# Twenty-four slot tiles of a mixture-of-experts layer computed in pairs of one expert, with a transposed first layer

## The reference

```python
# xf: 2048 tokens x 256; E = 8 experts, hidden width H = 512, top 2; S = 2 shared experts
sh = gelu(einsum('nd,sdh->snh', xf, sw1) + sb1)
shared_out = (einsum('snh,shd->nd', sh, sw2) + sb2.sum(0)) / S
gates = xf @ router_w + router_b
topv, topi = top_k(gates, 2)
probs = softmax(topv)
comb = einsum('nke,nk->ne', one_hot(topi, E), probs)
h = gelu(einsum('nd,edh->enh', xf, w1) + b1[:, None, :])
y = einsum('enh,ehd->end', h, w2) + b2[:, None, :]
x = x + tanh(g_ffn) * (shared_out + einsum('ne,end->nd', comb, y))
```

## Time and profile before

| | us |
|---|---|
| median of 3 runs | 387.39 |
| least and most | 387.09, 388.18 |
| profiled execution | 387.97 |
| its span | 386.1 |
| TensorE busy in it | 379.8 |
| VectorE, ScalarE, GpSimd busy | 280.9, 249.4, 221.1 |

### The profile page before, as it was taken

One profiled execution on the slowest core, in us unless ns is written; L12 is line 12 of the kernel. 1 busy time (PEld: TensorE's weight loads), 2 busy tenths in 40 slices (PEclk: granted clock), 3 DMA queues, 4 the chain that ended last, 5 costly groups with the idle time before them and its releaser, 6 DMA issues.

```text
span 386.1 us, 9097 instructions
## 1 busy us (share of the span) xinstructions
PE 379.8 (98%) x2725; PEld 354.3 (92%) x2726; DVE 280.9 (73%) x627; ACT 249.4 (65%) x600; POOL 221.1 (57%) x261
## 2 busy tenths in 40 slices
PE   8999999999999999999999999999999999999996
PEld 7898989999999899999999989999999999999995
DVE  5798799988988998797889885445554455445386
ACT  2766545646755635888869757776667666777850
POOL 8366656788788762577872345555555555552200
PEclk9999999999999999999999999999999999999999
DMA  7990000001000066003930112222222222221397
GB/s 230 306 321 3 2 14 29 16 22 33 14 14 27 17 230 247 14 4 70 274 98 1 36 49 70 83 70 83 69 82 73 78 71 79 75 75 42 87 355 254
DMA packets 32539, 35.89 MB, mean 93 GB/s; under 512 B 9531, under 2 KB 26365, under 8 KB 32509
## 3 DMA queue, kind: packets, MB, share of 16 engines
q1 hardware_dynamic: 27664, 25.21, 21.9%
q0 software_dynamic: 4768, 10.28, 8.7%
q10 hardware_dynamic: 76, 0.02, 0.0%
HBM read 25.79 MB, written 9.59 MB: 92 GB/s over the span
## 4 chain that ended last, share of the span: by engine, by line
PE 92%; DVE 3%; POOL 2%; ACT 1%; issue 1%; DVEq 0%; POOLq 0%
PE psum L1348 14%; PE psum L1395 13%; PE psum L1206 12%; PE psum L1229 11%; PE psum L1166 10%; PE psum L1122 9%; PE psum L1414 4%; PE psum L1089 3%; PE psum L1337 2%; PE psum L1008 2%; PE psum L1046 2%; PE psum L1070 2%; PE psum L1154 1%; PE psum L988 1%; PE psum L1186 1%
## 5 line engine op out<-in xcount | busy, mean ns | idle before, releaser
L1883 DVE COPY hs<-psum 128x512 f32<-128x512 f32 x39 | 27.0, 691 | 56.4 <-PE psum L1395 56.4
L681 POOL DMA_INDIRECT xsl<-y_rows,table x39 | 38.3, 982 | 47.5 <-PE psum L1337 36.2
L688 POOL DMA_INDIRECT y_tok<-ysl,table x39 | 38.6, 990 | 31.8 <-ACT ysl L949 31.5
L966 ACT ACTIVATE hr<-psum,b_cur 128x128 f32<-128x128 f32 x156 | 44.4, 372 | 3.0 <-DVE hr_lo L1873 1.2
L662 POOL DMA_INDIRECT names<-named,pos x32 | 37.8, 1181 | 12.8 <-issue 7.9
L949 ACT ACTIVATE ysl<-psum,table 128x256 f32<-128x256 f32 x39 | 18.5, 475 | 38.7 <-PE psum L1348 38.7
L615 POOL TENSOR_TENSOR Eb<-Eb,rinv 128x512 f32<-128x512 f32 x32 | 33.5, 1065 | 13.1 <-DVE rinv L1604 13.1
L825 ACT ACTIVATE yTb<-psum 128x256 f32<-128x256 f32 x16 | 6.2, 385 | 42.6 <-PE psum L1186 42.6
L1348 PE MATMUL psum<-w_hi,hr_hi 128*128 x156 | 28.0, 301 | 0.0
L1873 DVE TENSOR_TENSOR hr_lo<-hr,hr_hi 128x512 fp32r<-128x512 f32 x39 | 26.6, 682 | 1.8 <-ACT hr_hi L970 1.8
L1395 PE MATMUL psum<-w_hi,xsT_hi 128*128 x78 | 27.6, 436 | 0.0
(11 more groups left out here) (248 smaller groups left out, 1169.7 us busy)
## 6 DMA issues: line engine op xcount, KB each, us to landing
w_raw<-in_L_ffn_w SPq DMA_DIRECT2D x2, 4096.0 KB, 18.1
y_got<-y_tok SPq DMA_DIRECT2D x8, 512.0 KB, 7.6
xs_all<-in_x SPq DMA_DIRECT2D x4, 512.0 KB, 12.3
sw_raw<-in_L_ffn_sw SPq DMA_DIRECT2D x2, 1024.0 KB, 13.9
y_rows<-ybuf SPq DMA_DIRECT2D x16, 128.0 KB, 1.7
out<-xs_all SPq DMA_DIRECT2D x3, 512.0 KB, 3.2
wq_sb<-in_L_xattn_Wq SPq DMA_DIRECT2D x2, 512.0 KB, 6.5
wo_sb<-in_L_xattn_Wo SPq DMA_DIRECT2D x1, 1024.0 KB, 14.2
```

The lines of the kernel that those rows point to most:

```text
L681: nc.gpsimd.indirect_dma_start(xsl[:, s % 2, :], None, y_rows, bass.IndirectOffsetOnAxis(ap=table[:, s, 0:1].bitcast(I32), axis=0)).then_i ...
L688: nc.gpsimd.indirect_dma_start(y_tok, bass.IndirectOffsetOnAxis(ap=table[:, s, 1:2].bitcast(I32), axis=0), ysl[:, s % 2, :], None).then_in ...
L966: last = nc.scalar.activation(hr[:, m, :], bank[4 + par][:, m * P:(m + 1) * P], ACT.Gelu, bias=b1_cur[:, par, m:m + 1])
```

## The change

The slot tiles are sorted otherwise: 15 single tiles and 24 tiles in 12 pairs ("doubles") whose two tiles belong to one expert. Six singles run first, then the 12 doubles, then nine singles. `entry(s)` gives the place in the tables.

In a double:

- TensorE takes w1 as the fixed operand and the turned x of both tiles (256 columns) as the moving one, so that h comes out transposed and needs no turn: 24 matmuls (L1586), no transposes of h, no hs copy. x of both tiles is turned into one bank by 4 transposes (`turn_wide`, L1479). The second layer of the pair before takes 24 matmuls (`give_wide`, L1492), in two halves.
- The weights of the pair's expert are first copied by VectorE into w1_cur (`move_weights`, L2095; 128x1024 for the high and as much for the low part, two buffers), two doubles ahead.
- ScalarE makes four gelus of 128x256 in two halves; hr2 holds one half, so each half's rounded copy (`kept`) and low part (`half_left`) come before the next half's gelus.
- GpSimd's order is written out anew, with gathers up to three doubles ahead.

w1_cur lies where the low part of the shared experts' weights (sw_s[1]) was. SP writes this part to DRAM (2 MB, `sw_lo_kept`) ahead of the doubles and reads it back in four pieces at the end; TensorE waits for it before the late shared experts. The routing tables get the sorting into pairs, and their running sum stands behind `columns_rest(2)` now. A few semaphores are merged, and the counters are six instead of five.

```diff
+DOUBLES = (TOK * TOPK // P - E) // 2
+SINGLES = SLOT_TILES - 2 * DOUBLES
+DOUBLE0 = 6
+SINGLE1 = DOUBLE0 + 2 * DOUBLES
...
+        w1_cur = at_words("w1_cur", [P, 2, 2, KD, HID], AT_SW + 2 * SW_WORDS, F32R)
...
+            sp.wait_ge(sw_ready, SW_PIECES)
+            sp.dma_start(sw_lo_kept[:, :], sw_s[1][:, :].bitcast(F32)).then_inc(sw_moved, 16)
+
             sp.wait_ge(routed_all, 1)
...
+                n = s - (SLOT_TILES - BACK)
+                if n >= 0:
+                    sp.wait_ge(h_psum, SINGLE1 + n)
+                    piece = slice(n * 2 * SW_WORDS // BACK, (n + 1) * 2 * SW_WORDS // BACK)
+                    sp.dma_start(sw_s[1][:, piece].bitcast(F32), sw_lo_kept[:, piece]).then_inc(sw_moved, 16)
...
+            for d in range(1, DOUBLES):
+                for n in range(2):
+                    if d + 3 < DOUBLES:
+                        gather(tile_of(d + 3) + n)
+                    scatter(tile_of(d - 1) + n)
+                if d == DOUBLES - 2:
+                    for n in range(2):
+                        gather(SINGLE1 + n)
+                if d == DOUBLES - 1:
+                    gather(SINGLE1 + 2)
+            for s in range(SINGLE1 + 1, SLOT_TILES):
                 if s + 2 < SLOT_TILES:
                     gather(s + 2)
-                if s >= 3:
-                    scatter(s - 3)
+                scatter(s - 3)
...
+                def gelus(h):
+                    act.wait_ge(h_psum, s + (h + 1))
+                    act.wait_ge(ht_lo, s + h)
+                    for m in range(2):
+                        last = nc.scalar.activation(hr2[:, m, :], bank[2 + 2 * par + h][:, m * 2 * P:(m + 1) * 2 * P], ACT.Gelu,
+                                                    bias=b1_cur[:, par, 2 * h + m:2 * h + m + 1])
+                    last.then_inc(ht_raw, 1)
+
+                def kept(h):
+                    act.wait_ge(ht_raw, s + (h + 1))
+                    if d == 0:
+                        act.wait_ge(ye_psum, DOUBLE0 - 1 + h)
+                    elif h == 0:
+                        act.wait_ge(half_used, s - DOUBLE0)
+                    else:
+                        act.wait_ge(ye_psum, s)
+                    nc.scalar.activation(hr2_hi[:, 2 * h:2 * h + 2, :], hr2[:, :, :], ACT.Copy).then_inc(ht_hi, 1)
+
+                act.wait_ge(b1_ready, s + 2)
+                gelus(0)
+                if d == DOUBLES - 1:
+                    turned(SINGLE1, 0)
+                else:
+                    turned_wide(s + 2, 1 - par)
+                kept(0)
+                gelus(1)
+                kept(1)
+                output(s - 2, 0)
+                output(s - 1, 1)
...
+            def double(d, par, s, j):
+                pe.wait_ge(xt_lo, s + 2)
...
+                pe.wait_ge(w1_moved, s + (2 - DOUBLE0))
+                for m in range(HC):
+                    n, half = 0, m // 2
+                    for x_part, w_part in ((xsT2_hi, 0), (xsT2_hi, 1), (xsT2_lo, 0)):
+                        for k in range(KD):
+                            last = nc.tensor.matmul(bank[2 + 2 * par + half][:, (m % 2) * 2 * P:(m % 2 + 1) * 2 * P],
+                                                    w1_cur[:, par, w_part, k, m * P:(m + 1) * P],
+                                                    x_part[:, k, :], start=(n == 0), stop=(n == 3 * KD - 1))
+                            n += 1
+                    if m % 2 == 1:
+                        last.then_inc(h_psum, 1)
...
+            def move_weights(par, n):
+                nc.vector.tensor_copy(w1_cur[:, par, n, :, :],
+                                      w1_s[n][:, at(expert(2 + par)), :, :].rearrange("p a k n -> p (a k) n").bitcast(F32)
+                                      ).then_inc(w1_moved, 1)
...
+                if d == 0:
+                    move_weights(1, 1)
+                half_left(0)
+                if more:
+                    dve.wait_ge(h_psum, s + 2)
+                    move_weights(par, 0)
+                half_left(1)
+                if more:
+                    move_weights(par, 1)
```

## The result

The changed kernel took 394.46 us (median of 4, 391.98 to 399.48) beside 387.24 (387.02 to 388.18) of the kernel before: a ratio of 1.016, 95% interval 1.0122 to 1.0198. The ratio leaves out the longest execution, which counts as a slow one. The kernel is slower by 1.6%, where 386.0 and a range of 381.5 to 391.0 were forecast. The profiled execution took 391.98, its span is 390.2; against the profiled execution of before that is 4.0 more, where the sum said 1.4 less. The other executions are longer still; how far the traces explain that is told at the end.

The account below looks back on a forecast made before the run. TensorE, busy 98% of the span, was taken as the bound. 387.97 - 9.6 + 1.1 + 4.8 + 0.8 + 1.2 + 0.3 = 386.6, less 0.58 to the median: 386.0 us, range 381.5 to 391.0.

Parts of the forecast that it names:

- hole of 4.8 us: Leaving the doubles: TensorE waits 4.8 us for tile 30's gather, which stands behind two scatters on GpSimd; bounds 4.0 to 5.8.
- the landing of tile 7's gather: Entering the doubles: the gather lands 2.8 us after its start, making TensorE wait +0.3 us.
- the three waits behind the hole: After the doubles: outputs of 26 and 27 +0.8, gather of 32 +0.5, first singles +0.7 us; together 1.0 to 2.8.
- What bounds the kernel: Kernel before: TensorE, busy 98% of the span, 3.48 us per slot tile; an edit pays by shortening its list.
- Part 1: TensorE's list in a double: a pair falls from 6.98 to 6.18 us, gaining 9.6 us over 12 doubles.
- Part 2: Whether another engine sets the doubles' period of 6.18 us: none is full, costed at nothing.
- copy and circle: In doubles: weights' copy 0.69 us, ScalarE-VectorE circle through hr2 5.76 with it, 0.4 to spare; 6.29 with a 1.22 copy.
- The collision: Rival in the doubles: weights' copies and GpSimd's DMAs delay each other, the circle becomes the bound; 391 us, chance 0.23.
- Part 3: Entering the doubles: +0.3 us for tile 7's gather, +0.8 for a late copy of weights; +1.1, bounds 0.6 to 1.5.
- Part 4: Leaving the doubles: GpSimd's order makes a 4.8 us wait for tile 30, then further waits of 0.8, 0.5 and 0.7.
- Part 5: Ahead of routed tiles: longer routing tables delay w2's load by 1.35 us, ScalarE's wait 4.6; +0.3, bounds 0 to 1.5.
- the fall of the clock: Rival behind the hole: TensorE's clock drops to 1.2 GHz after the idle time; 388.4 us, at most 390.7, chance 0.15.

Follow-up runs that it names:

- after_again: The changed kernel, unchanged, run and profiled again: 392.97 us, 1.012 of the kernel before.
- hole_filled_b: Changed kernel plus 52 unread TensorE transposes where it waits for tile 30, gather as late: 390.46 us, 1.007 of the kernel before.
- all_three: gathers_first plus gather of 32 earlier, outputs of 28 and 29 later, two weight copies elsewhere on VectorE: 383.22 us, 0.9876 of kernel before; 401.49 on a slower chip.
- gathers_first: Changed kernel with GpSimd's gathers of tiles 30 and 31 ahead of the scatters of 24 and 25: 402.95 us on a slower chip, 385.89 when rerun elsewhere.

## Why the prediction was wrong, step by step

Three steps of the prediction failed. The largest was left at nothing: the sum has a hole of 4.8 us and takes the clock behind it as 1.00. The other two were sized too small: the landing of tile 7's gather at the entrance, and the three waits behind the hole.

- **What bounds the kernel**: right. TensorE's list was the bound before, and it is in the doubles.
- **Part 1**, the list of a double: right, 6.19 against 6.18 and 0.12 for a matmul, but the last digit is luck. Four transposes of x take 0.35 and not 0.28, as the four transposes of h had shown (272.07 to 272.43, 0.36), and the second layer 2.96 and not 3.02. The gain is 12 x (6.96 - 6.19) = 9.2 instead of 9.6, since a tile had cost 3.48, not 3.49.
- **Part 2**, copy and circle: right. The copies took 0.70 and 0.71, estimated 0.69; the reserve was 0.27, estimated 0.4. The collision, the rival on the slower side, cost TensorE nothing, though it can be seen on GpSimd: four DMAs that began while a copy ran (234.70, 243.54, 259.25, 263.38) took 1.09 to 1.27 in place of 0.96 to 0.98, and ended 0.8 to 0.9 after the copy. The copies never took more than 0.745, also those that began with or just before a scatter. GpSimd gave way and had the slack for it, as the prediction's argument against this rival said. The rule of the Trainium skill in "SBUF — State Buffer", section "SBUF: two separate sides", would have made the two exclude each other for a whole instruction. The trace agrees for a DMA that begins during a copy; it does not for a copy that begins together with a DMA (265.34 for both, copy 0.72, scatter 0.98).
- **Part 3**, the entrance, +1.1: too small. By distances of starts 1.6 for the gather of tile 7 (predicted 0.3), 0.9 for the copy (0.8) and 0.4 at 260.0: 2.9. The 0.7 that TensorE waited there for a copy is the only wait that the profile names inside the twelve doubles, and part 3 had costed it. The term that failed is the landing: I took the median of 2.8 where the row gave 4.2 as the longest, and it was 4.0 at the one gather that had no reserve; with the packet of instructions at another time, in after_again, there was no wait at all.
- **Part 4**, the way out: the hole right in place, cause and size, 4.9 between starts against 4.8, each station of GpSimd as computed (314.95, 316.21, 317.47, where the end of double 10 at 312.53 and the computed 2.33, 3.61, 4.89 make 314.86, 316.14, 317.42). The three waits behind it came to 3.3 by distances of starts (0.6, 0.45, 1.9 and 0.3 in small pieces at the singles after) against 2.0: ScalarE's output of tile 29 needed the scatter of tile 27 to land, 3.86 us after its issue, and nothing in my chain had scatters landing.
- **Part 5**, the front: the delay was 2.07 in place of 1.35, and it cost nothing; TensorE reaches the same place at 230.20, 230.24 before. The load of w2, issued 2.07 later, was there 1.3 sooner (197.28 against 198.58), so ScalarE's wait was 2.06 where 4.6 was named as a sign; why the load was faster stays open.
- **The rivals**: this is where the time went wrong. The forecast took the hole and left the clock at 1.00, and put the fall of the clock apart, at 0.15. But the hole was in the forecast itself, so the fall was not a rival to it but its next step. It cost 1.9 us in the profiled execution (from 320.31 to 325.32 are 5.0 for work that took 3.1 in hole_filled_b) and more in others, as the second fall in after_again shows, another 1.2. The profile of before could not show it, as the prediction said; the page that it cited, "TensorE: Matmul & The Clock Gate", Part 1, in the Trainium skill, stated it, and both profiles agree with it now (0.74 granted in the stretch with the hole, 1.00 with the hole filled).

The sum again, for the profiled execution: -9.2 + 2.9 + 4.9 + 1.9 + 3.3 = +3.8, measured 4.0. Against the forecast's -1.4 the difference is 5.4: 1.9 the clock, 1.8 the entrance, 1.3 the first singles, 0.4 the gain, 0.1 the hole, less 0.3 at the front; 0.2 stays unassigned.

The median moved by 7.2 and not by 4.0, since the profiled execution was the shortest of the changed kernel (2.5 below its median) and a long one of the kernel before (0.7 above). No trace shows what the other three executions lost. Their granted clocks do say something: 0.99 at 391.98, 0.983 at 394.06 and 394.86. A mean clock lower by 0.007 over 390 us is an estimated 2.7 us, which fits these two. For the longest, 399.48 at 0.981, the same estimate gives 3.6 of the 7.5 us; the rest is open.

## What to carry to other kernels

Where a gain of 9 us is spread over a loop and the program is written anew at its two ends, the ends decide: walk each queue through them, the landing of scatters included, and put loads that open the next part ahead of stores that close the last one. A gap in TensorE like this one, 4.7 us, should be costed with the half clock behind it as one term, and a variant that leaves waits of 1 to 2 us close together is worth a look at the granted clock in more than one execution. And a circle of waits that has 0.3 us of reserve is a bound in waiting, whatever the busy shares say.

## What the runs showed of the hardware that was not expected

- An idle time of 4.7 us was followed by some 4 us at half clock; with TensorE kept busy by idle transposes the clock stayed, and the median was 2.5 us lower.
- In one execution of the same kernel two waits of 1.2 and 1.7 us, 2.6 us apart by their ends, were followed by a second fall, in another waits of 0.3 and 1.6 were not. Executions of the kernel spread from 390.5 to 393.5 with granted clocks of 0.994 to 0.985.
- A GpSimd DMA that begins while VectorE copies within SBUF ends 0.8 to 0.9 us after the copy, with two sources as with one: 1.09 to 1.27 beside copies of 0.69, 1.4 to 1.9 beside those of 1.22, in place of 0.96 to 0.98. The copy is not lengthened, also where it begins 0.46 us into the DMA (1.22).
- One of a gather's sixteen parts can land 0.8 to 2.0 us behind the other fifteen (240.74 against 239.47; 241.88 against 239.90): in eleven of eleven traces with a 16 KB packet of instructions 1.3 to 2.7 us behind the gather's issue, and in neither of the two with the packet at 0.6 or earlier.
- A copy of 128x1024 words within SBUF took 0.70 us on VectorE where the same amount with two sources took 1.22.
- Two of the chips ran the kernel before 1.2 to 1.6% slower and the changed kernel's variants 2.4 to 4.8% slower than elsewhere (all_three 401.5 against 383.2), with some signals of TensorE recorded 1 us and more late, in gathers_first at a clock of 1.00.
